# Router pieces moved from the scan into the attention, second scores ahead of the next keys, reciprocals copied by VectorE

## The reference

```python
# 1. selective state space layer: 16 states for each of 256 channels
u = silu(causal_conv4(x @ W_in[:, :256]) + conv_b);  res = x @ W_in[:, 256:]
delta = softplus((u @ W_x)[..., :64] @ W_dt + b_dt);  Bm, Cm = the other 2 x 16 columns
h[t] = exp(delta * A) * h[t-1] + delta * Bm[t] * u[t]      # for each of 16 states
x = layernorm(x + ((h . Cm) + u * D) * silu(res) @ W_out)
# 2. attention on a context, 16 heads of 8, causal, rotary positions
x = layernorm(x + softmax(rope(q) @ rope(k).T / sqrt(8) + masks) @ v @ Wo.T + bo)
# 3. mixture of 8 experts, 2 for each token, hidden size 512
logits = x @ gate_w.T; the two largest, their gates (0.02 threshold)
x = layernorm(x + sum over the two of gate * (silu(x @ w1[e].T) * (x @ w3[e].T)) @ w2[e].T)
```

## Time and profile before

| | us |
|---|---|
| median of 3 runs (lowest, highest) | 1181.85 (1177.59, 1184.74) |
| the profiled execution: its time, its span | 1183.17, 1181.4 |
| span of the eight groups, scans and attentions | from about 37 to 870 |
| the experts and the last loop | from about 893 to the end |
| PE busy | 987.5 (84%) |
| DVE busy | 850.3 (72%) |
| ACT busy | 725.3 (61%) |
| POOL busy | 544.0 (46%) |

### The profile page before, as it was taken

The page is one execution under the profiler, slowest core; times in us unless marked ns, Lnnn a source line. Parts: engine busy times, 40 slices in busy tenths (PEclk is TensorE's granted clock), DMA queues, the critical chain, the costliest instruction groups (busy, mean ns, idle before and its releaser), DMA issues. The chain is left out here.

```text
span 1181.4 us, 18995 instructions
## 1 busy us (share of the span) xinstructions
PE 987.5 (84%) x5175; PEld 544.5 (46%) x5176; DVE 850.3 (72%) x1681; ACT 725.3 (61%) x2029; POOL 544.0 (46%) x372
## 2 busy tenths in 40 slices
PE   6799889979988997998899778876946999999920
PEld 2345534544453454445345434432534666666610
DVE  1697799779779967986996798699653544444466
ACT  3668857866885786588578656944742444444420
POOL 2564357356725734672564457356212332323324
PEclk9899999989999998999999889999987999999975
DMA  4000000000100000010000000000421111111133
GB/s 111 9 1 27 2 1 19 28 1 1 46 1 1 16 30 2 0 44 3 1 14 24 1 1 28 1 1 2 159 90 51 40 41 45 40 40 45 40 116 116
DMA packets 39400, 36.54 MB, mean 31 GB/s; under 512 B 6561, under 2 KB 35361, under 8 KB 38945
## 3 DMA queue, kind: packets, MB, share of 16 engines
q1 hardware_dynamic: 33792, 25.99, 7.7%
q0 software_dynamic: 4352, 8.99, 2.1%
q10 hardware_dynamic: 1184, 0.70, 0.3%
HBM read 23.99 MB, written 11.67 MB: 30 GB/s over the span
## 5 line engine op out<-in xcount | busy, mean ns | idle before, releaser
L409 POOL TENSOR_TENSOR scan<-du,w 128x1024 f32<-128x1024 f32 x128 | 300.7, 2355 | 279.2 <-ACT w L555 177.6
L818 DVE TENSOR_TENSOR_SCAN scan<-bank,scan 128x512 f32<-128x512 f32 x240 | 284.6, 1206 | 2.9 <-ACT bank L567 2.7
L567 ACT ACTIVATE bank<-delta,a_neg 128x512 f32<-128x512 f32 x240 | 165.7, 691 | 124.0 <-DVE scan L818 122.8
L1299 PE MATMUL y_ps<-w,ident 128*128 128x512 f32 x480 | 234.2, 611 | 0.0
L473 POOL DMA_INDIRECT y<-aoT,dest x72 | 69.6, 966 | 172.3 <-DVE aoT L1142 168.0
L824 DVE TENSOR_TENSOR w<-scan,bank 128x1024 f32<-128x1024 f32 x120 | 143.3, 1194 | 3.3 <-issue 1.9
L1299 PEld LDWEIGHTS y_ps<-w,ident 128*128 128x128 f32 x480 | 93.2, 194 | 77.1 <-issue 62.5
L1101 DVE TENSOR_TENSOR zpos<-zabs,bank 128x512 f32<-128x512 f32 x74 | 51.0, 689 | 79.8 <-PE bank L1571 79.8
L1289 PE MATMUL bank<-bc,sel 96*128 96x512 bf16 x128 | 50.5, 395 | 57.2 <-DVE w L824 53.9
L555 ACT ACTIVATE w<-bank 128x512 f32<-128x512 f32 x121 | 70.7, 584 | 39.5 <-PE bank L1280 39.1
L602 ACT ACTIVATE prob<-y_ps,nmax 128x128 f32<-128x128 f32 x256 | 91.5, 436 | 0.0
(11 more groups left out here) (247 smaller groups left out, 1860.4 us busy)
## 6 DMA issues: line engine op xcount, KB each, us to landing
qk<-xg SPq DMA_DIRECT2D x79, 65.0 KB, 1.9
cn<-in_ctx SPq DMA_DIRECT2D x8, 256.0 KB, 2.9
mask_b<-in_mask SPq DMA_DIRECT2D x8, 256.0 KB, 3.1
w<-in_w1T SPq DMA_DIRECT2D x1, 2048.0 KB, 9.3
w<-in_w3T SPq DMA_DIRECT2D x1, 2048.0 KB, 7.5
prob<-in_w2T SPq DMA_DIRECT2D x1, 2048.0 KB, 7.8
u<-y SPq DMA_DIRECT2D x4, 512.0 KB, 4.7
w<-in_x SPq DMA_DIRECT2D x6, 256.0 KB, 3.0
```

What stands on the lines that cost most here:

```text
L409: g_.tensor_tensor(bu[:, n % 3], du[:, :, :], b_row[:, n % 3, :].unsqueeze(1).broadcast_to((P, 2, T)), ALU.mult).then_inc(s["bu_sb"], 1)
L567: A(bank[(6 if n else 4) + h], delta[:, h, :], ACT.Exp, scale=a_neg[:, h, n:n + 1]).then_inc(s["a_ps"], 1)
L818: v_.tensor_tensor_scan(hst[:, n % 3, h, :], bank[(6 if n else 4) + h], bu[:, n % 3, h, :], 0.0, ALU.mult, ALU.add).then_inc(s["h_sb"], 1)
L1299: last = MM(y_ps[:, h], ident[:, :], hc[:, n % 3, h, :], start=False, stop=False, skip_group_check=True)
```

## The change

- All router pieces of `w` up to `ranked` move from the scan of `m` into its attention: `best` behind the first layer norm, `which` ahead of the first maxima, `cast` and `mark` into part 1, `ranked` (now with the update of `base`, step 6 of the links) into the head of part 3. PE's `ranks` stand ahead of `head_t` in part 3, and its result lies in other columns of bank 1.
- `spots`, `spot_sum` and `spots_out` stand in step 1 of the next scan, and so the scatter comes one group later: `scatter(m - 2)` at the end of scan `m`, and two scatters behind the last attention.
- In part 0 of the attention PE makes `scores(g, 1, 0)` ahead of `keys(e, 0, 0)`.
- DVE copies the transposed reciprocals of parts 0 to 2 itself; ACT copies those of part 3 alone.

The diff, cut to its core:

```diff
@@ POOL
             def b_low(m, n):
-                at(pool, "scat", (m - 2) * 2 * S * 16)
+                at(pool, "scat", (m - 3) * 2 * S * 16)
...
                 masks(m)
-                if w is not None:
-                    scatter(w)
+                if m >= 2:
+                    scatter(m - 2)
...
+            scatter(G - 2)
             scatter(G - 1)
@@ ACT, attention
                 for t in range(S):
-                    if t:
-                        rdenT_out(g, t - 1)
                     pT_out(g, t, 0)
@@ DVE
             def normed(g, t):
+                if t < S - 1:
+                    at(dve, "rdenT_ps", S * g + t + 1)
+                    v_.tensor_copy(rdenT[:, t % 2], bank[(t + 1) % 2][:, 2 * P:3 * P]).then_inc(s["rdenTd_sb"], 1)
+                    at(dve, "rdenTd_sb", (S - 1) * g + t + 1)
+                else:
+                    at(dve, "rdenT_sb", g + 1)
                 at(dve, "pv_ps", S * g + t + 1)
-                at(dve, "rdenT_sb", S * g + t + 1)
...
                     states(m, n, 0)
+                    if n == 1 and m >= 2:
+                        spots(m - 2)
+                        spot_sum(m - 2)
+                        spots_out(m - 2)
                     if n == 1 and w is not None:
                         normed(w, S - 1)
...
+                if w is not None:
+                    best(w)
                 rope_q(g, 0)
                 add_q(g, 0)
+                if w is not None:
+                    which(w)
...
                 for t in range(S):
+                    if t == S - 1 and w is not None:
+                        ranked(w)
+                        normed(g, t - 1)
...
                     pT_out(g, t, 1)
+                    if t == 1 and w is not None:
+                        cast(w)
+                        mark(w)
...
             w = G - 1
+            spots(w - 1)
+            spot_sum(w - 1)
+            spots_out(w - 1)
@@ PE
             def heads_v(g, t):
                 if t:
-                    at(pe, "rdenT_sb", S * g + t)
-                if t >= 2:
-                    at(pe, "aoT_sb", S * g + t - 1)
+                    at(pe, "aoT_sb", S * g + t)
+                if t == S - 1 and g:
+                    at(pe, "route", 8 * (g - 1) + 6)
...
-                        if n == 8:
-                            ranks(w)
...
-                    keys(e, 0, 0)
                 for t in range(S):
                     if t + 1 < S:
                         scores(g, t + 1, 0)
+                    if t == 0 and e is not None:
+                        keys(e, 0, 0)
                     if t:
                         inverses_t(g, t - 1)
                         heads_v(g, t - 1)
+                    if t == S - 1 and w is not None:
+                        ranks(w)
                     head_t(g, t, 0)
```

More of the change, by code:

```diff
@@ L954, in ranked @@
             def ranked(w):
-                rk = bank[1][:, 2 * S * E:(3 * S + 1) * E].rearrange("p (s e) -> p s e", e=E)
+                rk = bank[1][:, 3 * P:3 * P + (S + 1) * E].rearrange("p (s e) -> p s e", e=E)
                 at(dve, "rank_ps", w + 1)
                 step(w, 5, TT(rank[:, :, :], rk[:, 0:S, :], base[:, :].unsqueeze(1).broadcast_to((P, S, E)), ALU.add))
+                at(dve, "route", LINKS * w + 5)
+                step(w, 6, TT(base[:, :], base[:, :], rk[:, S, :], ALU.add))
             def spots(w):
                 b = slice(w * S, w * S + S)
-                at(dve, "route", LINKS * w + 5)
-                step(w, 6, TT(base[:, :], base[:, :], bank[1][:, (3 * S) * E:(3 * S + 1) * E], ALU.add))
+                at(dve, "route", LINKS * w + 6)
                 step(w, 7, TT(prk[:, :, :, :], rank[:, :, :].unsqueeze(2).broadcast_to((P, S, 2, E)), oh_all[:, b, :, :], ALU.mult))
@@ L987, in _ @@
                     times_c(m, n - 1)
-                    if w is not None:
-                        if n == 6:
-                            which(w)
-                        if n == 7:
-                            mark(w)
-                        if n == 9:
-                            ranked(w)
-                        if n == 10:
-                            spot_sum(w)
                     states(m, n, 1)
@@ L1003, in _ @@
                             second_norm(w)
-                        if n == 5:
-                            best(w)
-                        if n == 6:
-                            cast(w)
-                        if n == 9:
-                            spots(w)
-                        if n == 10:
-                            spots_out(w)
                     if n == 4 and e is not None:
@@ L1043, in _ @@
                         widen(g, t)
-                    if t:
+                    if t and not (t == S - 1 and w is not None):
                         normed(g, t - 1)
                     pT_out(g, t, 1)
+                    if t == 1 and w is not None:
+                        cast(w)
+                        mark(w)
                     if t == 0 and e is not None:
@@ L1252, in low_steps @@
                 else:
-                    at(pe, "route", 8 * (m - 2) + 6)
+                    at(pe, "lg_sb", m - 1)
                 for h in range(2):
@@ L1278, in row_b @@
                 if n == 3:
-                    at(pe, "rdenT_sb", S * m)
+                    at(pe, "rdenT_sb", m)
                 MM(bank[1 if n < 3 else 0], sel[:, n, :], bc3[:, m % 2, :], start=True, stop=True).then_inc(s["b_ps"], 1)
@@ L1325, in values @@
                 else:
-                    at(pe, "route", 8 * (g - 1) + 6)
+                    at(pe, "lg_sb", g)
                 for t in range(S):
@@ L1446, in ranks @@
                 for t in range(S + 1):
-                    o = bank[1][:, (2 * S + t) * E:(2 * S + t + 1) * E]
+                    o = bank[1][:, 3 * P + t * E:3 * P + (t + 1) * E]
                     for r in range(t):
```

2 lines of the change are left out of this document (1 added, 1 removed).

## The result

| | before | after |
|---|---|---|
| median of 4 runs, us (lowest, highest) | 1181.99 (1177.59, 1184.74) | 1143.01 (1140.69, 1145.19) |
| the profiled execution's span, us | 1181.4 | 1143.4 |
| PE, DVE, ACT, POOL busy, us | 987.5, 850.3, 725.3, 544.0 | 973.0, 848.5, 718.4, 542.5 |

The ratio is 0.9693, with a 95% interval of 0.966 to 0.9725.

A forecast was written before the change was run, and what follows sets the result against it. DVE sets the scan's pace with PE close behind; in the attention DVE, PE and ACT wait in turn. Terms -22.0 + 0.5 - 10.3 + 1.7 + 3.4 = -26.7 us from 1183.17 gave 1156.5, forecast 1155 us, range 1147 to 1168.

The forecast's parts named there:

- rival 3: PE keeps its clock, without the 1.2 GHz stretches in step 1: 8 us less, 1147 us; chance 0.11.
- Router pieces, -22.0: Router pieces leave the scan, where nothing covers them: seven scans shorter by 3.15 us each, -22.0 us.
- PE's lag, +0.5: In the scan, some 1.8 us of PE's lag behind DVE cost nothing; +0.1 us in five groups booked, +0.5 us.
- Rival 1: PE takes over the scan with steps of 3.87 against 3.36 us: 1162 us; chance 0.13.
- Scores ahead of keys, -10.3: In attention part 0, `head_t` starts 1.47 us earlier, in seven attentions: -10.3 us.
- The same pieces in the attention, 0: Router pieces moved into the attention stand where engines wait anyway, so they cost zero.
- Rival 2: `which` in the attention is held up by POOL's product, in seven groups: +8.8 us, 1164 us; chance 0.07.
- Reciprocals by DVE, 0: In the attention, ACT without three copies a group only waits for PE, DVE's copies fill idle time: 0 us.
- Step 1, +1.7: `spots`, `spot_sum`, `spots_out` ahead of `normed` in the next scan: up to 0.57 us late, half of six scans, +1.7 us.
- The end, +3.4: Behind the last attention, `pos` of group 7 must wait for group 6's scatter, delaying the experts' token loads: +3.4 us.
- Rival 4: PE loses its clock more often in the groups; three more stretches for each group give 1201 us; chance 0.03.
- Rival 5: The gains meet other waits, above all in part 0 and the end; half remains: 1168 us; chance 0.06.

The follow-up runs named there:

- before_fill_ranks: Kernel before plus three small unread matmuls per group on PE, ahead of `head_t` in part 3, where the change puts the ranks: median 1173.86 us, ratio 0.993.
- before_warm: Kernel before plus small unread matmuls where PE waits, at the attention's end and in steps 1 and 3 of the scan: median 1169.72 us, ratio 0.9927.
- router_again: Kernel before with only the router pieces moved, PE's ranks in bank 2, rerun on another chip: median 1155.77 us, ratio 0.9769.
- warm_pe_load: Changed kernel with small unread matmuls where PE waits, plus two more row matmuls in each of steps 5 to 10 of every scan: median 1156.95 us, ratio 0.9802.
- copies_only: Kernel before with only the reciprocals of parts 0 to 2 copied by DVE: median 1208.56 us, ratio 1.0027 to the kernel before.
- after_act_copies: Changed kernel with ACT's copies of the reciprocals as before, ranks in bank 2: median 1166.8 us, ratio 0.9692 to the kernel before.
- warm_keys_first: Changed kernel with small unread matmuls where PE waits, but first keys again ahead of the second scores: median 1151.44 us, ratio 0.9748 to the kernel before.
- the filled kernels: Kernels before and after, each with small unread matmuls where PE waits, at the attention's end and in scan steps 1 and 3: medians 1169.72 and 1140.99 us.

## Why the prediction was wrong

**The step that failed is the sum's silence on PE's clock.** I gave it zero in the sum and 8 us, with a chance of 0.11, as rival 3. In the profiled pair it was 11.0 us, and by the medians between 7 and 12. The evidence stood in my own rows: the earlier trace rows show the statistics waiting 2.50 us in group 2, and the earlier trace rows the wait of 1.44 us ahead of it. I even wrote that the ranks fill some of that gap. What I did not do was take the change's own matmuls, 0.7 us put into the gap that is followed by the loss, as a term. before_fill_ranks shows that 0.8 us of matmuls there bring 10.2 us in before. I also priced a stretch from the one wait that I saw (2.2 us) and not from the lengths of scans in the trace of before: 61.5, 62.5 and 64.1 us for equal work say that there is a term. They do not give its size, 16.2 us, since each of the seven scans has a stretch; the clean 59.8 us came only from before_warm.

**Router pieces, -22.0:** a scan without stretches went from 59.82 to 56.79 us, 3.03 each, 21.2 in all (router_again has the same 56.80). The forecast was 3.15.

**PE's lag, +0.5:** measured 0.05 to 0.07 in each of five scans, about 0.3. The size held, the reason was half wrong: 1.8 us of lag are not free (warm_pe_load). Rival 1 did not come true, but nothing stood between it and the changed kernel.

**Scores ahead of keys, -10.3:** 1.36 to 1.40 for each attention, 9.7 us. The forecast was 1.47; the other 0.6 us of the attentions' 10.3 lie in the last attention (0.2) and in tenths of the seven others (the next two terms).

**The same pieces in the attention, 0:** nearly right. router_again has attentions of 42.09 to 42.35 against 42.09 in before, 0.6 us in all seven. `cast` took 0.16 and `mark` 0.23 us. Rival 2 falls: each FIND_INDEX8 took 0.16 us, beside a POOL product too. The exclusion for two SBUF inputs in the Trainium skill ("SBUF — State Buffer", the section on SBUF's two sides) does not show for it; but each search stands in the trace as two instructions, MATCH_VALUE_LOAD and FIND_INDEX8, so I may have read a rule for two inputs onto instructions that have one each. `mark`, a product of two tiles, agrees with the rule: in before it took 0.76 us and ended at 173.48, when POOL's L409 (171.05 + 2.36 = 173.41) ended.

**Reciprocals by DVE, 0:** nearly right. copies_only has a first attention of 42.09, and after_act_copies 40.73 us, where after has 40.72. With the router pieces in the attention the copies do give something: 42.10 to 42.35 us in router_again against 41.92 to 42.21 in warm_keys_first, 0.13 to 0.18 each from the second on, 0.9 in all. ACT's copy at 220.00 waits 0.40 us for PE where the copy was.

**Step 1, +1.7:** measured 0.6 us in each of six scans (56.79 against 57.39), 3.5 in all. I had halved it since half of the groups had PE at 1.2 GHz and a wait that would hide it. The mechanism held. Scans 1 and 2 of the filled kernel before are equal (59.81, 59.82), so the 0.6 us are these pieces. With the clock kept there was nothing to hide them, as the same missing term would have told.

**The end, +3.4:** 1.3 us. `pos` of group 7 waited 0.51 us for the scatter of group 6, not 3.4. That scatter took 11.7 us from its `pos` (829.31) to the end of the wait, where I had put 13.4 (the way to the tokens' load, which is longer than to the landing), and the last chain itself took longer: its logits were waited for 3.77 us instead of 2.72 (DVE at 837.06), which hid some more: `pos` comes 1.57 us later behind the last `normed` than before, and the logits alone 0.97.

**The sum:** -21.2 + 3.5 - 10.3 + 1.3 = -26.7 us (PE's lag is in the first term), against my -26.7 and the 26.4 us between the filled kernels. That it agrees to the tenth is luck: step 1 came out 1.8 us dearer than forecast and the end 2.1 cheaper. With the clock's -11.0 it is -37.7 of the 38.0 us; the beginning (-1.2) and the stretch behind the load (+1.0), in which nothing was changed, nearly cancel.

**Rival 4**, more stretches, falls: there were fewer. **Rival 5**, gains that meet other waits, falls with the sum.

**What stays open:** why one chip has half-clock stretches of 10.2 us at the attentions' beginning, in the kernels traced there, and another has none; which piece of the remaining 5 us in after falls where, since it moved between two runs; what the clock costs in the executions that were not profiled, whose times spread over 12 us for before; and whether the ranks by themselves keep the clock in the changed kernel.

## What to carry to other kernels

Where a stage repeats, compare its lengths before anything else: if equal work takes 61.5, 62.5 and 64.1 us, as here, the excess is a term of its own (and the shortest of them need not be free of it), and every change that adds to or takes from PE's gaps ahead of it has to be priced with it. Moving small matmuls into the gap ahead of such a loss can be worth more than the time they free where they stood. And an engine that is close behind the one that sets the pace has its slack set by its tightest consumer (here ACT's), not by the one that is looked at first. And where a kernel's own executions spread over 1%, as before's did here, one pair of profiles gives the places of a loss, not its size for the median.

## What was not expected of the hardware

- More work for PE made the program shorter: 0.8 us of products that nobody reads, in each group, gave 0.7% (ratio 0.993 [0.9897, 0.9963]); the fillers at four places gave the same 0.7% (0.9927 [0.9899, 0.9955]).
- In two profiles of before, taken at different times, the stretches of half clock in scans 1 to 5 began within 0.4 us of each other (155.8 and 155.5, 244.6 and 244.2, and so on) and lasted the same 3.4 or 6.8 us; in two of after they moved.
- `cast` took 0.97 us beside POOL's product and 0.16 where POOL was idle; searches beside a POOL product took 0.16 us or less.
- POOL issued one indirect DMA each 1.26 us, and eight of them ahead of the last eight cost the end nothing, since POOL then waited 1.4 to 1.9 us for the last `pos`.
